# Cross-attention, 16 batches: 292 columns of each low part and the tail copies moved to GpSimd, whose program is written turn by turn

## The reference

```python
q = (pre_q @ Wq + bq).reshape(b, ql, H, D_Q)
k = (pre_k @ Wk + bk).reshape(b, kl, H, D_Q)
v = (pre_k @ Wv + bv).reshape(b, kl, H, D_Q)
scores = jnp.einsum('bqhd,bkhd->bhqk', q, k) / jnp.sqrt(jnp.float32(D_Q))
attn = jax.nn.softmax(scores, axis=-1)
ctx = jnp.einsum('bhqk,bkhd->bqhd', attn, v).reshape(b, ql, H * D_Q)
out = ctx @ Wo + bo
x = pre_q + out
mu = jnp.mean(x, axis=-1, keepdims=True)
var = jnp.mean(jnp.square(x - mu), axis=-1, keepdims=True)
return (x - mu) * jax.lax.rsqrt(var + EPS) * gamma + beta
```

## Time and profile before

| what | value |
|---|---|
| median of 3 runs | 908.91 us (907.51 to 912.77) |
| the profiled execution: its own time | 911.81 us |
| its span, first to last instruction | 909.9 us |
| TensorE busy | 882.5 us, 97% of the span |
| VectorE busy | 814.9 us, 90% |
| ScalarE busy | 746.3 us, 82% |
| GpSimd busy | 327.0 us, 36% |
| granted TensorE clock, mean | 0.993 of full speed |

### The profile page before, as it was taken

The page is one execution under the profiler, slowest core; times in us unless marked ns, Lnnn a source line. Parts: engine busy times, 40 slices in busy tenths (PEclk is TensorE's granted clock), DMA queues, the critical chain, the costliest instruction groups (busy, mean ns, idle before and its releaser), DMA issues.

```text
span 909.9 us, 25457 instructions
## 1 busy us (share of the span) xinstructions
PE 882.5 (97%) x10366; PEld 674.6 (74%) x10366; DVE 814.9 (90%) x1041; ACT 746.3 (82%) x1082; POOL 327.0 (36%) x385
## 2 busy tenths in 40 slices
PE   7799999999999999999999999999999999999996
PEld 6477777777777777777777777777777777777776
DVE  4799799999998999999899999989999899998983
ACT  3677868888888888888888888888888888888883
POOL 3032496434415234242514434143442435243011
PEclk9899999999999999999999999999999999999999
DMA  8598978999999999999999999999999999999995
GB/s 232 112 190 168 196 158 184 218 207 185 216 211 205 209 210 213 197 201 222 204 209 208 209 210 219 207 194 208 213 221 207 198 217 200 205 197 211 203 178 113
DMA packets 683065, 181.17 MB, mean 199 GB/s; under 512 B 654596, under 2 KB 682052, under 8 KB 682948
## 3 DMA queue, kind: packets, MB, share of 16 engines
q1 hardware_dynamic: 681332, 178.48, 103.7%
q10 hardware_dynamic: 1344, 0.53, 0.2%
q0 software_dynamic: 272, 0.53, 0.2%
HBM read 15.35 MB, written 0.82 MB: 18 GB/s over the span
## 4 chain that ended last, share of the span: by engine, by line
PE 34%; DVE 18%; ACT 15%; SPq 14%; DMA 11%; issue 8%; POOL 0%; POOLq 0%; ACTq 0%; DVEq 0%
PE ps L532 14%; PE ps L546 10%; DMA pt_lo<-p_lo 9%; DVE p_lo L767 8%; ACT p L861 6%; SPq L331 5%; DVE nmax L752 5%; PE ps L551 5%; ACT p_hi L869 5%; SPq L339 4%; PE ps L400 2%; ACT o_t L884 2%; DVE rsum L758 1%; SPq L323 1%; DMA pt_hi<-p_hi 1%
## 5 line engine op out<-in xcount | busy, mean ns | idle before, releaser
L869 ACT ACTIVATE p_hi<-p,rinv 128x1444 f16<-128x1444 f32 x200 | 299.8, 1499 | 89.3 <-DVE rinv L760 87.4
L767 DVE SCALAR_TENSOR_TENSOR p_lo<-p,rinv,p_hi 128x1444 f16<-128x1444 f32 x200 | 349.9, 1749 | 13.5 <-DMA pt_lo<-p_lo 10.7
L752 DVE TENSOR_REDUCE nmax<-ps 128x1 f32<-128x1446 f32 x200 | 329.8, 1649 | 8.7 <-PE ps L532 8.7
L861 ACT ACTIVATE p<-ps,nmax 128x1446 f32<-128x1446 f32 x200 | 291.7, 1459 | 26.3 <-DVE nmax L752 25.4
L546 PE MATMUL ps<-pt_hi,c_hi 128*128 128x128 f16 (+1 forms) x2288 | 268.7, 217 | 3.6 <-ACT o_t L884 3.1
L546 PE MATMUL ps<-pt_hi,c_lo 128*128 128x128 f16 (+1 forms) x2288 | 268.6, 217 | 0.0
L546 PEld LDWEIGHTS ps<-pt_hi,c_hi 128*128 128x128 f16 x2288 | 216.8, 98 | 34.4 <-ACT o_t L884 14.5
L546 PEld LDWEIGHTS ps<-pt_hi,c_lo 128*128 128x128 f16 x2288 | 217.0, 98 | 17.9 <-issue 0.2
L532 PE MATMUL ps<-ct_hi,g_hi 128*128 128x482 f16 (+3 forms) x624 | 157.1, 370 | 2.2 <-DMA ct_hi<-c_hi 2.2
L551 PE MATMUL ps<-pt_lo,c_hi 128*128 128x128 f16 (+1 forms) x2288 | 157.0, 217 | 0.0
L532 PE MATMUL ps<-ct_hi,g_lo 128*128 128x482 f16 (+3 forms) x624 | 156.8, 369 | 0.0
(11 more groups left out here) (109 smaller groups left out, 716.9 us busy)
## 6 DMA issues: line engine op xcount, KB each, us to landing
c_raw<-in_ctx_dram SPq DMA_DIRECT2D x32, 256.0 KB
pt_hi<-p_hi SPq DMA_TRANSPOSE x200, 3.5
pt_lo<-p_lo SPq DMA_TRANSPOSE x200, 3.8
c_raw<-in_ctx_dram SPq DMA_DIRECT2D x16, 192.0 KB
c_raw<-in_ctx_dram SPq DMA_DIRECT2D x48, 18.0 KB
out_dram<-late_sb SPq DMA_DIRECT2D x16, 50.0 KB
x_sb<-in_x_dram SPq DMA_DIRECT2D x1, 600.0 KB
o_t<-in_L_xattn_Wq_dram SPq DMA_DIRECT2D x2, 256.0 KB, 4.5
```

The source lines that it names most:

```text
L752: dve.tensor_reduce(nmax[:, n % RING:n % RING + 1], ps[:, bank:bank + 3, 0:KEYW], AX.XY, ALU.max, negate=True).then_inc(s_nm, 1)
L767: dve.scalar_tensor_tensor(out=p_lo[:, par, 0:KL], in0=p32[:, n % P32S, 0:KL], scalar=rinv[:, i:i + 1], in1=p_hi[:, par, 0:KL], op0=ALU.mu ...
L861: act.activation(p32[:, n % P32S, :].rearrange("p (k w) -> p k w", w=KEYW), ps[:, bank:bank + 3, 0:KEYW], ACT.Exp, bias=nmax[:, i:i + 1], ...
L869: act.activation(p_hi[:, par, 0:KL], p32[:, n % P32S, 0:KL], ACT.Copy, scale=rinv[:, i:i + 1]).then_inc(s_hi, 1)
```

## The change

GpSimd gets the last 292 columns of each tile's low part (columns 1152 to 1443) from VectorE, and the tail copies from ScalarE. Its piece, `lo_share(n)`, is three instructions: scale 292 columns of `p32` into a new buffer `p_scaled`, copy the tail twice from `p_hi` behind the low part, subtract `p_hi` from `p_scaled`. It begins when VectorE's part of the same tile is done (`s_lo`), and signals `s_lq`. SyncE's `transpose_lo` and ScalarE's `exponentials` two tiles on now also wait for `s_lq`. GpSimd's program no longer goes by windows but by turns, `lo_share(n - 1)` first, then at most a few of its old pieces. `transpose_context_lo` moves from r = 8 to r = 9.

```diff
--- before.py
+++ after.py
@@ -49,6 +49,7 @@
     P32S = 2
+    SHARE = 9 * P
     UNSCALES = 4
@@ -60,7 +61,7 @@
     CT_HI_AT = 7
-    CT_LO_AT = 8
+    CT_LO_AT = 9
     CT_LO_AT_FIRST = 9
@@ -150,6 +151,7 @@
+        p_scaled = sb("p_scaled", [P, KL - SHARE])
...
             def transpose_lo(n):
                 par = n % 2
                 sp.wait_ge(s_lo, n + 1)
+                sp.wait_ge(s_lq, n + 1)
                 sp.wait_ge(s_pt, n + 1)
...
-                dve.scalar_tensor_tensor(out=p_lo[:, par, 0:KL], in0=p32[:, n % P32S, 0:KL], scalar=rinv[:, i:i + 1],
-                                         in1=p_hi[:, par, 0:KL], op0=ALU.mult, op1=ALU.subtract).then_inc(s_lo, 1)
+                dve.scalar_tensor_tensor(out=p_lo[:, par, 0:SHARE], in0=p32[:, n % P32S, 0:SHARE], scalar=rinv[:, i:i + 1],
+                                         in1=p_hi[:, par, 0:SHARE], op0=ALU.mult, op1=ALU.subtract).then_inc(s_lo, 1)
...
                 if n >= P32S:
                     act.wait_ge(s_lo, n - P32S + 1)
-                    act.wait_ge(s_pt, n - P32S + 1)
+                    act.wait_ge(s_lq, n - P32S + 1)
...
                     act.wait_ge(s_th[par], halves(n - 2))
+                    act.wait_ge(s_pt, n - 1)
                 act.activation(p_hi[:, par, 0:KL], p32[:, n % P32S, 0:KL], ACT.Copy, scale=rinv[:, i:i + 1]).then_inc(s_hi, 1)
-
-            def hi_tail(n):
-                par, i = n % 2, n % RING
-                if n > 1:
-                    act.wait_ge(s_tl[par], halves(n - 2))
-                tail = p32[:, n % P32S, (KT - 1) * P:KL].unsqueeze(1).to_broadcast([P, 2, KTAIL])
-                act.activation(p_lo[:, par, KL:KL + 2 * KTAIL].rearrange("p (i k) -> p i k", i=2), tail, ACT.Copy,
-                               scale=rinv[:, i:i + 1]).then_inc(s_pt, 1)
...
                 hi_part(n)
-                hi_tail(n)
...
+            def lo_share(n):
+
+                par, i = n % 2, n % RING
+                pool.wait_ge(s_lo, n + 1)
+                if n > 0:
+                    pool.wait_ge(s_lq, n)
+                pool.tensor_scalar(p_scaled[:, :], p32[:, n % P32S, SHARE:KL], rinv[:, i:i + 1], 1.0, ALU.mult,
+                                   ALU.mult).then_inc(s_qs, 1)
+                if n > 1:
+                    pool.wait_ge(s_tl[par], halves(n - 2))
+                tail = p_hi[:, par, (KT - 1) * P:KL].unsqueeze(1).to_broadcast([P, 2, KTAIL])
+                pool.tensor_copy(p_lo[:, par, KL:KL + 2 * KTAIL].rearrange("p (i k) -> p i k", i=2), tail).then_inc(s_pt, 1)
+                pool.wait_ge(s_qs, n + 1)
+                pool.tensor_tensor(p_lo[:, par, SHARE:KL], p_scaled[:, :], p_hi[:, par, SHARE:KL],
+                                   ALU.subtract).then_inc(s_lq, 1)
...
-            for w in range(B):
-                b = w + 1
-                    query_scales(b)
-                    for g in range(NG):
-                        split_queries(b, g)
...
+            for n in range(N + 1):
+                if n >= 1:
+                    lo_share(n - 1)
+                if n == N:
+                    break
+                w, r = window(n)
+                b, g_at = w + 1, G_AT if w else G_AT_FIRST
                 if b < B:
-                    query_scales(b)
...
+                    if r == g_at - 1:
+                        query_scales(b)
+                    elif g_at <= r < g_at + NG:
+                        split_queries(b, r - g_at)
+                    if r - 1 in CHI_AT:
+                        context_lo(b, CHI_AT.index(r - 1), left_before(n))
+                g = n - A16_AT - 1
+                if 0 <= g < NG:
+                    pool.wait_ge(s_16h, g + 1)
+                    heads = slice(HG * g, HG * g + HG)
+                    leave_lo(g, a_sb[:, heads, :], a16[:, heads], ax_scale[:, 0:1], NT)
+                elif n == XRES_AT:
...
+                g = n - X16_AT - 1
+                if 0 <= g < NX:
...
                 if w > 0:
-                    inverse_deviation(w - 1)
-                    scale_rows(w - 1)
+                    if r == ROWS_AT + 1:
+                        inverse_deviation(w - 1)
+                    elif r == ROWS_AT + 2:
+                        scale_rows(w - 1)

```

More of the change, by code:

```diff
@@ L226, in cross_attention_kernel @@
         s_lo = sem("p_lo_ready")
+        s_qs = sem("p_share_scaled")
+        s_lq = sem("p_lo_share_ready")
         s_th = [sem(f"p_hi_transposed{i}") for i in range(2)]
@@ L256, in cross_attention_kernel @@
         X16_AT = 18
+        XRES_AT = X16_AT
         WARM_UP = 12
@@ L957, in context_tail, with context_lo @@
                 pool.tensor_copy(c_tail[0:2 * KTAIL, par, :], c_hi[0:2 * KTAIL, par, KT - 1, :]).then_inc(s_chl, 1)
-            def context_lo(b):
-                par = b % 2
+            def context_lo(b, g, left):
+                par, tiles = b % 2, slice(TG * g, TG * g + TG)
                 pool.wait_ge(s_al, b + 1)
-                for g in range(NT):
-                    tiles = slice(TG * g, TG * g + TG)
-                    if NT * b + g > NT:
-                        pool.wait_ge(s_cl, NT * (b - 1) + g)
-                    pool.tensor_scalar(c_scaled[:, :], c_raw[:, par, tiles, :].rearrange("p t d -> p (t d)"),
-                                       alpha[:, par:par + 1], 1.0, ALU.mult, ALU.mult).then_inc(s_cs, 1)
-                    pool.wait_ge(s_cs, NT * (b - 1) + g + 1)
-                    pool.wait_ge(s_chi, NT * b + g + 1)
-                    pool.tensor_tensor(c_lo[:, par, tiles, :].rearrange("p t d -> p (t d)"), c_scaled[:, :],
-                                       c_hi[:, par, tiles, :].rearrange("p t d -> p (t d)"), ALU.subtract).then_inc(s_cl, 1)
-                pool.wait_ge(s_cl, NT * b)
-                context_tail(b)
+                if NT * b + g > NT:
+                    pool.wait_ge(s_cl, NT * (b - 1) + g)
+                if left:
+                    pool.wait_ge(s_16, left)
+                pool.tensor_scalar(c_scaled[:, :], c_raw[:, par, tiles, :].rearrange("p t d -> p (t d)"),
+                                   alpha[:, par:par + 1], 1.0, ALU.mult, ALU.mult).then_inc(s_cs, 1)
+                pool.wait_ge(s_cs, NT * (b - 1) + g + 1)
+                pool.wait_ge(s_chi, NT * b + g + 1)
+                pool.tensor_tensor(c_lo[:, par, tiles, :].rearrange("p t d -> p (t d)"), c_scaled[:, :],
+                                   c_hi[:, par, tiles, :].rearrange("p t d -> p (t d)"), ALU.subtract).then_inc(s_cl, 1)
+                if g == NT - 1:
+                    pool.wait_ge(s_cl, NT * b)
+                    context_tail(b)
             def inverse_deviation(b):
@@ L992, in scale_rows, with leave_lo @@
                 pool.tensor_tensor(y[:, par, :], zg[:, par, :], rows_b[0:QL, 2, :], ALU.add).then_inc(s_y, 1)
-            def leave_lo(i, raw, parts, scale):
+            def leave_lo(i, raw, parts, scale, groups):
                 n, w = raw.shape[1], raw.shape[2]
                 at = c_scaled[:, 0:n * w].rearrange("p (n w) -> p n w", w=w)
+                pool.wait_ge(s_cl, groups)
                 if i:
@@ new lines, in left_before @@
+            def left_before(n):
+                return min(max(n - A16_AT - 1, 0), NG) + min(max(n - X16_AT - 1, 0), NX)
+            for n in range(N + 1):
[5 more added lines that the diff above has]
+                b, g_at = w + 1, G_AT if w else G_AT_FIRST
+                if b < B:
+                    if r == g_at - 1:
[10 more added lines that the diff above has]
+                elif n == XRES_AT:
+                    emptied(pool, J_R)
+                    emptied(pool, J_X3)
+                    pool.wait_ge(s_ax, 2 * NG)
+                    pool.tensor_tensor(x_sb[:, :, :], x_sb[:, :, :], rows_b[0:QL, 0:1, :].to_broadcast([QL, B, D]),
+                                       ALU.add).then_inc(s_xres, 1)
+                g = n - X16_AT - 1
+                if 0 <= g < NX:
+                    pool.wait_ge(s_16h, NG + g + 1)
+                    batches = slice(XG * g, XG * g + XG)
+                    leave_lo(NG + g, xT[:, batches, :], x16[:, batches], ax_scale[:, 1:2],
+                             NT + sum(1 for c in CHI_AT if WHOLE + c + 1 <= n))
```

18 lines of the change are left out of this document (removed).

## The result

| | before | after |
|---|---|---|
| median, us (range, runs) | 908.28 (907.51 to 912.77, 4) | 933.09 (931.67 to 938.56, 4) |
| profiled execution, us | 911.8 (span 909.9) | 931.67 (span 929.8) |
| mean granted TensorE clock | 0.993 | 0.985 |

The ratio is 1.0273, 95% interval 1.0232 to 1.0314: the change costs 25 us. I had predicted 916, range 903 to 928. The sign was right, the size and the main reason for it were not.

The account below looks back on a forecast made before the run. It took TensorE as the bound, VectorE within a few per cent. Terms -6 - 1 + 1.5 + 6.5 + 6 summed to +7 us, giving 916 against the median of 908.9; range of 8 in 10, 903 to 928.

Parts of the forecast that it names:

- Pieces of 1.5 us on GpSimd, low part 1.41: Per tile, GpSimd's scaling, tail copy and subtraction take 1.5 us together (1.4 to 1.9); VectorE's shortened `lo_part` takes 1.41.
- Mutual exclusion: GpSimd's instructions and VectorE's `lo_part` exclude each other; GpSimd's time per turn includes one `lo_part`, counted as 1.2 us.
- The moved transpose, +6.5: `transpose_context_lo` behind two more issues makes TensorE wait 0.9 us in each of seven windows: 6.5 us, bounds 0 to 14.
- Steady waits, -6: VectorE and ScalarE run further ahead of TensorE, removing 6 of its 8.6 us of waits from turn 25 on.
- slow landings, +1.5: Low transposes leave 1.5 us later; slow ones hold up `lo_part`, 0 to 4 us in all, taken as 1.5.
- My 4.5 us of room for a landing: The low transpose's buffer is wanted again two turns after, 4.5 us behind its issue; landing takes 3.8, at most 6.8.
- Window 1, +6: In turns 13 to 23 GpSimd ends 10.6 us late; TensorE's waits grow, net 2 to 9 us, taken as 6.
- covered in steady turns: ScalarE's exponential waiting for `s_lq` has 1.4 us to spare in plain turns and 2.3 in 4.65 us turns.
- Window 0 and the end, -1: In window 0 and after the last scores, where ScalarE's work gets shorter, 1 us is gained.
- faster: Engines run ahead and the context transpose lands in time, if share(8) ends before 6.9 us into turn 9: 904; chance 0.22.
- Saturation: GpSimd and `lo_part` saturate, above 3.0 us a turn: 934 half way, 965 in full; chance 0.13.

Follow-up runs that it names:

- the tails alone: Kernel before with GpSimd's program by turns and tail copies moved to GpSimd, VectorE making the whole low part, context transpose at r = 8: 900.56 us.
- The share at ct 8: The changed kernel with the low context's transpose back at r = 8, 292 columns and tail copies still on GpSimd: 919.43 us, ratio 1.0102.
- three buffers: The changed kernel with the low context's transpose back at r = 8 and three `p_lo` buffers instead of two: 910.76 us, ratio 1.0034.
- the turn program: Kernel before with only GpSimd's program written turn by turn, no columns or tail copies moved, context transpose at r = 8: 907.42 us, ratio 0.9975.
- the early scaling at ct 9: The changed kernel, context transpose at r = 9, with GpSimd's scaling starting at the inverse of the row's sum, not behind VectorE's low part: 915.96 us.
- the early version: The changed kernel with context transpose at r = 8 and GpSimd's scaling starting at the inverse of the row's sum: 907.25 us, ratio 0.9992.

## Why the prediction was wrong

Point by point, in its own order.

- **Pieces of 1.5 us on GpSimd, low part 1.41**: right (0.51, 0.24, 0.75; 1.41 where free, mean 1.52). The Trainium skill, GPSIMD Engine Reference, section 4.1 Engine selection, warns of a factor of about two; here VectorE gave up 0.3 us and GpSimd took 0.51 + 0.75 = 1.26 for the same columns, a factor of four: the one instruction of VectorE became two, and the subtraction alone takes 0.75.
- **Mutual exclusion**: right (the tail copy took 1.30 beside the low part, free 0.29). The Trainium skill, SBUF — State Buffer, section Who interferes with whom, calls it an exclusive lock; the trace agrees.
- **The moved transpose, +6.5**: the step that failed. Its sum laid scores, row maximum, low part and share end to end and had the low part of tile 8 end 4.9 us into turn 9. The trace of before shows it ending at 7.1; two rows of VectorE there, in window 8, turn 9 beginning at 505.97:

```profile
509.76 1.65 DVE L752 TENSOR_REDUCE nmax<-ps 128x1 f32<-128x1446 f32 x1
511.33 1.71 DVE L767 SCALAR_TENSOR_TENSOR p_lo<-p,rinv,p_hi 128x1444 f16<-128x1444 f32 x1
```

  VectorE runs 2 us behind TensorE, and I gave it 0.3. The low context was also wanted at 14.1, not 13.75 (the first low-context matmul of that turn is the old batch's), and in those seven windows of before it landed 4.2 us after its issue on average, not 3.7. From 6.85, where the low part ends in them on average: less 0.3, plus the share's 1.5, plus 0.8 for the context's tail, is 8.9 (measured 8.7), the issue at 11.9 (12.0), the landing at 16.1 (16.0), a wait of 2.0, seven times 14 us (13.7). The wait could have been forecast from the trace. (7 x 0.9 is 6.3; the sum has 6.5.) The 3.5 us of slow restarts and 5.1 of the lower clock stood in no term, though the earlier trace rows showed such a fall and I named it for window 1.
- **Steady waits, -6, and slow landings, +1.5**: the two terms belong to different halves of the change. With the tails alone the waits from turn 25 on are 6.4 us less (8.6 to 2.2), about what I took; the likely reason is not that engines run ahead but that ScalarE no longer waits for a landing. The share at ct 8 puts 9.3 back (2.2 to 11.5), where I had at most 4, and three buffers take 6 of them away again: the loop. My 4.5 us of room for a landing let the transpose leave 0.1 us after the share; at ct 8 it leaves 0.6 after it on average, and 2.2 where the loads of the context stand ahead of it in SyncE's queue, and it lands 4.1 after its issue and not 3.8. VectorE waits 20.9 of its 49.8 us in the one turn of each window that this reaches.
- **Window 1, +6**: 3.3 measured. The parts are the turn program -2.1, the tails -2.0, the share +7.3, each read from one execution. GpSimd's backlog did reach TensorE there: ScalarE waited 3.61 us for a share before the exponential at 139.94, and TensorE behind it 3.04 us, up to 141.55:

```profile
139.94 1.47 ACT L867 ACTIVATE p<-ps,nmax 128x1446 f32<-128x1446 f32 x1 [3.61 <-POOL p_lo L942]
...
141.55 1.38 PE L538 MATMUL ps<-ct_hi,g_hi 128*128 128x482 f16 x3 [3.04 <-ACT p L867]
```

  Nearly all of ScalarE's 10.4 us of waits for the share lie in window 1; after it there is one of 0.3, so "covered in steady turns" was right.
- **Window 0 and the end, -1**: right (-2.1, -0.2, +1.1).
- **The rivals**: the point of "faster" was share(8) ready before 6.9; the early scaling at ct 9 has it at 7.1, still waits 6.8 us for `ct_lo` and is 6.9 us slower than before; at ct 8 it has it at 6.7 and is as fast as before. Saturation did not happen: GpSimd is busy 60% and stands idle 324.6 us waiting for the low part. It is late, not full.

In all: the sum had the moved step at 6.5 us, and the trace has 21.6 for its seven turns (22.5 less 0.9); that is more than the whole miss, and the other terms together came out 2 us under theirs. What remains open is the smaller split: how much of the share's remaining 6 us in the early version is exclusion and how much the loop was not separated.

The version that beats both kernels has GpSimd's turn program and its tail copies, no share, ct 8: 900.56 us, 0.74% (0.52 to 0.96) faster than before.
